# Cross attention of a Perceiver block: the spread as two rounded products, another order at the beginning, and one weight remainder on another engine

## What is computed

```python
x = x + xattn(layernorm(x), ctx)                 # x [32, 32, 512], ctx [32, 257, 512]
# inside xattn, 16 heads of 32:
q = x @ Wq + bq;  k, v = split(context @ Wkv + bkv)
q = larope(q);  k = larope(k)                    # rotation by position
scores = einsum('bhqd,bhkd->bhqk', q, k) * SCALE
attn = softmax(scores)                           # over 257 keys
out = einsum('bhqk,bhkd->bhqd', attn, v)         # back to [B, Lq, H * hd]
return out @ Wo + bo
```

## Time and profile before

| | us |
|---|---|
| median of 3 runs | 824.0 (823.18 to 825.72) |
| the profiled execution | 833.83 |
| its span, first to last instruction | 831.8 |
| PE busy in the span | 773.6 (93%) |
| VectorE, ScalarE, GpSimd busy | 459.1, 342.9, 211.7 |

### The profile page before, as it was taken

How to read it: one execution, slowest core, us unless ns; L and a number is a source line. 1 busy time by engine, 2 the same in 40 slices (tenths; PEclk the granted TensorE clock), 3 DMA queues, 4 the chain that set the end, 5 groups by cost and what they waited for, 6 DMA issues and landing times. The chain is left out here.

```text
span 831.8 us, 21082 instructions
## 1 busy us (share of the span) xinstructions
PE 773.6 (93%) x8896; PEld 645.1 (78%) x8897; DVE 459.1 (55%) x1005; ACT 342.9 (41%) x815; POOL 211.7 (25%) x194
## 2 busy tenths in 40 slices
PE   5889999999999999999999999999799996899980
PEld 4778888888898888888988888886577774678760
DVE  5645554554545546445555455555699985711115
ACT  6414335343353344433533445343466662123320
POOL 1212211231122212311232123121322220135540
PEclk9969999999999999999999999999899998589995
DMA  9503000010011000100010000213722329234438
GB/s 319 225 2 152 29 27 28 30 50 27 27 32 47 27 28 27 52 27 28 27 52 27 27 27 27 102 53 130 328 103 115 139 82 392 78 110 155 153 122 315
DMA packets 22249, 78.01 MB, mean 94 GB/s; under 512 B 3208, under 2 KB 3592, under 8 KB 19216
## 3 DMA queue, kind: packets, MB, share of 16 engines
q1 hardware_dynamic: 18480, 64.65, 20.9%
q0 software_dynamic: 3680, 12.06, 4.3%
HBM read 58.09 MB, written 18.61 MB: 92 GB/s over the span
## 5 line engine op out<-in xcount | busy, mean ns | idle before, releaser
L153 PE MATMUL bank<-chi,wparts 128*128 128x258 f32 x512 | 149.5, 292 | 7.6 <-DVE wparts L609 7.5
L154 PE MATMUL bank<-clo,wparts 128*128 128x258 f32 x512 | 145.3, 284 | 0.0
L155 PE MATMUL bank<-chi,wparts 128*128 128x258 f32 x512 | 145.3, 284 | 0.0
L153 PEld LDWEIGHTS bank<-chi,wparts 128*128 128x128 f32 x512 | 97.2, 190 | 20.4 <-issue 12.8
L314 POOL TENSOR_TENSOR ksin<-kb,const 128x1032 f32<-128x1032 f32 x32 | 95.1, 2971 | 62.8 <-ACT kb L373 62.8
L730 PE MATMUL bank<-wparts,chi 128*128 128x512 f32 x256 | 106.1, 414 | 0.2 <-DVE wparts L592 0.2
L731 PE MATMUL bank<-wparts,chi 128*128 128x512 f32 x256 | 101.5, 397 | 0.0
L732 PE MATMUL bank<-wparts,clo 128*128 128x512 f32 x256 | 101.3, 396 | 0.0
L320 POOL TENSOR_TENSOR pdiag<-pr,const 128x128 f32<-128x128 f32 x32 | 13.1, 410 | 340.7 <-ACT pr L381 340.7
L366 ACT ACTIVATE chi<-craw 128x1032 fp32r<-128x1032 f32 x32 | 34.1, 1066 | 157.3 <-PE bank L732 151.1
L154 PEld LDWEIGHTS bank<-clo,wparts 128*128 128x128 f32 x512 | 97.7, 191 | 0.0
(11 more groups left out here) (234 smaller groups left out, 1620.9 us busy)
## 6 DMA issues: line engine op xcount, KB each, us to landing
craw<-ctx_t_dram SPq DMA_DIRECT2D x32, 516.0 KB, 3.5
expert_lo<-weights_dram SPq DMA_DIRECT2D x8, 1024.0 KB, 12.0
expert_hi_scratch<-wraw SPq DMA_DIRECT2D x16, 512.0 KB, 2.6
wparts<-expert_hi_scratch SPq DMA_DIRECT2D x8, 1024.0 KB, 8.5
wraw<-weights_dram SPq DMA_DIRECT2D x7, 1024.0 KB, 6.7
expert_lo<-ffn_out_scratch SPq DMA_DIRECT2D x16, 256.0 KB, 4.6
x<-x_dram SPq DMA_DIRECT2D x8, 256.0 KB, 7.4
ffn_xn_scratch<-xn SPq DMA_DIRECT2D x8, 256.0 KB, 2.1
```

What stands on the lines that cost most here:

```text
L153: pe.matmul(psum, ahi(c), bhi(c), start=(c == 0), stop=False)
L154: pe.matmul(psum, ahi(c), blo(c), start=False, stop=False)
L155: last = pe.matmul(psum, alo(c), bhi(c), start=False, stop=(c == chunks - 1))
```

## The change

- The spread: the last probabilities and the inverse sums go into one tile `pair` of 128 x 8, VectorE splits it into a rounded part and a remainder (`pair_parts`), GpSimd's two diagonals are now those of the rounded part and of the remainder, each 128 x 256 of float32r, and PE adds two float32r products with a 0/1 matrix that GpSimd rounds once at the start (`same`).
- The beginning: VectorE first zeroes `kcos`, and PE makes 8 float32 products of 256 columns of it before its first work (`warm_up`). The first K goes chunk by chunk over all four parts, into four separate banks (`first_k_product`), and K's evacuations come after the roundings of Wq and Wv on ScalarE. Q and the first half of V wait chunk by chunk; both halves of V come before the transposes of rotated Q, whose halves are evacuated one by one. VectorE rotates Q before it makes kcos. SP issues Wv ahead of the bias of Q.
- The remainder of the output weight: not on GpSimd in batch 0 behind ksin, but on VectorE in batch 1, behind the remainder of transposed x (`w_lo(WO)`).
- Waits: the first exponential of a batch waits for the copies of `pair` in place of the diagonals; transposed Q counts two to a tile.

```diff
--- before.py
+++ after.py
...
     vlast = sb("vlast", [P, G, B])
-    pdiag = sb("pdiag", [P, 2, G, S])
+    pdiag = [sb(f"pdiag_{n}", [P, 2 * G, S], F32R) for n in ("hi", "lo")]
     olast = sb("olast", [P, G, S])
...
     rsum = sb("rsum", [P, G])
-    rinv = sb("rinv", [P, G])
+    pair = sb("p_last_and_rinv", [P, 2 * G])
+    pair_hi = sb("p_last_and_rinv_hi", [P, 2 * G], F32R)
+    pair_lo = sb("p_last_and_rinv_lo", [P, 2 * G])
+    same = sb("same_head", [P, P], F32R)
     pt = [sb(f"pt{i}", [P, 2 * P]) for i in range(G)]
...
     extra = score[3]
+    first_k = [proj[0], score[1], score[2], score[0]]
     av = quad[:, 3, 0:P]
...
     s_mask_rest = sem("mask_rest_in")
-    s_pdiag, s_spread, s_olast, s_osum, s_onorm = (sem(n) for n in (
+    s_pair_hi, s_pair_lo, s_same, s_pdiag, s_spread, s_olast, s_osum, s_onorm = (sem(n) for n in (
+        "p_last_and_rinv_hi_done", "p_last_and_rinv_lo_done", "same_head_rounded",
         "diagonals_done", "p_last_and_rinv_spread", "o_last_done", "o_sum_done", "o_normed"))
...
     sinq = const[:, C_SINQ:C_SINQ + 16].unsqueeze(1).to_broadcast([P, 2 * H, 16])
-    eye = const[:, C_EYE:C_EYE + S].unsqueeze(1).to_broadcast([P, G, S])
+    eye = const[:, C_EYE:C_EYE + S].unsqueeze(1).to_broadcast([P, 2 * G, S])
...
         weight(WQ)
+        weight(WV)
         bias_row(R_BQ, s_bq)
-        weight(WV)
         ctx(1, 1)
...
         def diagonals(b):
-            pool.wait_ge(s_exp, (b + 1) * G)
+            pool.wait_ge(s_pair_hi, b + 1)
             if not at_start(b):
                 pool.wait_ge(s_spread, b)
-            pool.tensor_tensor(pdiag[:, 0], pr[:, :, LK - 1].unsqueeze(2).to_broadcast([P, G, S]), eye, ALU.mult)
-            pool.wait_ge(s_rinv, b + 1)
-            pool.tensor_tensor(pdiag[:, 1], rinv[:].unsqueeze(2).to_broadcast([P, G, S]), eye,
+            pool.tensor_tensor(pdiag[0][:], pair_hi[:].bitcast(F32).unsqueeze(2).to_broadcast([P, 2 * G, S]), eye,
+                               ALU.mult)
+            pool.wait_ge(s_pair_lo, b + 1)
+            pool.tensor_tensor(pdiag[1][:], pair_lo[:].unsqueeze(2).to_broadcast([P, 2 * G, S]), eye,
                                ALU.mult).then_inc(s_pdiag, 1)
...
         pool.wait_ge(s_const, 16)
+        pool.tensor_copy(same[:], const[:, C_SAME:C_SAME + P]).then_inc(s_same, 1)
         ln_pool(pool, 0)
         k_sin(0)
-        def wo_lo():
-            pool.wait_ge(s_whi, WO)
-            pool.wait_ge(s_wlo, WO - 1)
-            pool.tensor_tensor(wlo[WO][:], wraw[WO % 2][:], whi[WO][:].bitcast(F32),
-                               ALU.subtract).then_inc(s_wlo, 1)
...
                     k_sin(b + 1)
-                if j == 0 and at_start(t):
-                    wo_lo()
...
                 act.wait_ge(s_ksin, b)
-            act.activation(kb[:, m, :], proj[m % 3][:, 0:LKP], ACT.Identity,
+            psum = first_k[m] if at_start(b) else proj[m % 3]
+            act.activation(kb[:, m, :], psum[:, 0:LKP], ACT.Identity,
                            bias=bias_cols[:, m:m + 1]).then_inc(s_kev, 1)
...
                 act.wait_ge(s_ptp, b * G)
-                act.wait_ge(s_pdiag, b)
+                act.wait_ge(s_rinv, 2 * b)
             act.activation(pr[:, g, 0:LK], sm[g][:], ACT.Exp, bias=nmax[:, g:g + 1], scale=-1.0,
...
         def qt_evac(t):
-            act.wait_ge(s_qtp, t + 1)
             if not at_start(t):
...
             for i in range(2):
+                act.wait_ge(s_qtp, 2 * t + i + 1)
                 act.activation(qt[i][:], score[2 + i].rearrange("p (g n) -> p g n", g=G),
...
         act.wait_ge(s_biask, 16)
-        k_evac(0, 0)
+        xt_hi(0)
         w_hi_chunks(WQ)
-        for m in range(1, 4):
+        w_hi_chunks(WV)
+        for m in range(4):
             k_evac(0, m)
-        xt_hi(0)
-        w_hi_chunks(WV)
         ctx_hi_at(0, 1)
...
             if not at_start(t):
-                dve.wait_ge(s_qtp, t)
+                dve.wait_ge(s_qtp, 2 * t)
             dve.tensor_tensor(qb[:], extra, bias[:, R_BQ, :], ALU.add).then_inc(s_qb, 1)
...
             if not at_start(b):
+                dve.wait_ge(s_pair_lo, b)
+            dve.reciprocal(pair[:, G:2 * G], rsum[:]).then_inc(s_rinv, 1)
+            dve.tensor_copy(pair[:, 0:G], pr[:, :, LK - 1]).then_inc(s_rinv, 1)
+        def pair_parts(b):
+            dve.wait_ge(s_rinv, 2 * b + 2)
+            if not at_start(b):
                 dve.wait_ge(s_pdiag, b)
-            dve.reciprocal(rinv[:], rsum[:]).then_inc(s_rinv, 1)
+            dve.tensor_copy(pair_hi[:], pair[:]).then_inc(s_pair_hi, 1)
+            dve.wait_ge(s_pair_hi, b + 1)
+            dve.tensor_tensor(pair_lo[:], pair[:], pair_hi[:].bitcast(F32), ALU.subtract).then_inc(s_pair_lo, 1)
...
                     dve.wait_ge(s_whi, n)
-                lo = dve.tensor_tensor(wlo[n][:, c, :], wraw[n % 2][:, c, :], whi[n][:, c, :].bitcast(F32),
-                                       ALU.subtract)
-            lo.then_inc(s_wlo, 1)
+                dve.tensor_tensor(wlo[n][:, c, :], wraw[n % 2][:, c, :], whi[n][:, c, :].bitcast(F32),
+                                  ALU.subtract).then_inc(s_wlo if c == KC - 1 else s_wklo, 1)
...
+        dve.memset(kcos[:], 0.0).then_inc(s_zero, 1)
         ctx_lo(0, 0)
...
         dve.wait_ge(s_x0, 16)
-        dve.wait_ge(s_zero, 1)
+        dve.wait_ge(s_zero, 2)
         ln(0, x[:, 0, :])
-        w_lo_chunks(WQ)
         dve.wait_ge(s_const, 16)
         xt_lo(0)
+        w_lo_chunks(WQ)
         w_lo_chunks(WV)
-        k_cos(0)
         dve.wait_ge(s_bq, 16)
         q_rope(0)
+        k_cos(0)
         ctx_lo(1, 1)
...
                 inverse_sums(b)
+                pair_parts(b)
                 if not (first and j == 0):
...
                     xt_lo(t + 1)
+                if j == 1 and first:
+                    w_lo(WO)
                 if j == 2 and not last:
...
+        def weight_chunk(n, c):
+            if c == KC - 1:
+                pe.wait_ge(s_wlo, n)
+            else:
+                pe.wait_ge(s_wklo, KC + (n - WQ) * (KC - 1) + c + 1)
         def q_product(t, b=None):
...
             mm3(pe, extra, lambda c: xthi[:, c, :], lambda c: xtlo[:, c, :],
-                lambda c: whi[WQ][:, c, :], lambda c: wlo[WQ][:, c, :]).then_inc(s_qmm, 1)
+                lambda c: whi[WQ][:, c, :], lambda c: wlo[WQ][:, c, :],
+                before=(lambda c: weight_chunk(WQ, c)) if at_start(t) else None).then_inc(s_qmm, 1)
...
             pe.wait_ge(s_qr, t + 1)
+            if at_start(t):
+                pe.wait_ge(s_kev, 3)
             if b is not None:
...
                     last = pe.transpose(score[2 + i][:, g * P:(g + 1) * P], a[:, g * P:(g + 1) * P], ident)
-            last.then_inc(s_qtp, 1)
-        def wk_chunk(c):
-            pe.wait_ge(s_wklo, c + 1)
+                last.then_inc(s_qtp, 1)
+        def warm_up():
+            pe.wait_ge(s_zero, 2)
+            for i in range(8):
+                pe.matmul(score[0][:, 0:2 * P], kcos[:, 0, 0:P], kcos[:, 1, 0:2 * P], start=True, stop=True)
+        def first_k_product():
+            pe.wait_ge(s_clo, 1)
+            for c in range(KC):
+                pe.wait_ge(s_wklo, c + 1)
+                for m in range(4):
+                    psum = first_k[m][:, 0:LKP]
+                    hi, lo = (a[:, c, m * P:(m + 1) * P] for a in (whi[WK], wlo[WK]))
+                    pe.matmul(psum, hi, chi[0][:, c, :], start=(c == 0), stop=False)
+                    pe.matmul(psum, hi, clo[0][:, c, :], start=False, stop=False)
+                    last = pe.matmul(psum, lo, chi[0][:, c, :], start=False, stop=(c == KC - 1))
+                    if c == KC - 1:
+                        last.then_inc(s_proj, 1)
...
                 pe.wait_ge(s_clo, b + 1)
-            if not (at_start(b) and m < 3):
-                if m == 0:
-                    pe.wait_ge(s_kev, b * 4)
-                elif m < 3:
-                    pe.wait_ge(s_vev, b * 2 - 2 + m)
-                else:
-                    pe.wait_ge(s_kev, b * 4 + 1)
+            if m == 0:
+                pe.wait_ge(s_kev, b * 4)
+            elif m < 3:
+                pe.wait_ge(s_vev, b * 2 - 2 + m)
+            else:
+                pe.wait_ge(s_kev, b * 4 + 1)
             mm3(pe, proj[m % 3][:, 0:LKP],
                 lambda c: whi[WK][:, c, m * P:(m + 1) * P], lambda c: wlo[WK][:, c, m * P:(m + 1) * P],
-                lambda c: chi[j % 2][:, c, :], lambda c: clo[j % 2][:, c, :],
-                before=wk_chunk if at_start(b) and m == 0 else None).then_inc(s_proj, 1)
+                lambda c: chi[j % 2][:, c, :], lambda c: clo[j % 2][:, c, :]).then_inc(s_proj, 1)
...
             psum = proj[(4 + u) % 3][:]
-            pe.wait_ge(s_kev, b * 4 + 2 + u)
+            if not at_start(b):
+                pe.wait_ge(s_kev, b * 4 + 2 + u)
             for c in range(KC):
+                if at_start(b) and u == 0:
+                    weight_chunk(WV, c)
```

(15 more changed lines are left out.)

## The result

The changed kernel takes 821.98 us (median of 20 runs, 818.03 to 824.69), the kernel before, measured with it on the same chip, 826.0 us (20 runs, 823.18 to 836.64). The ratio is 0.9942, 95% interval 0.9922 to 0.9962: about 4.8 us faster (the two medians are 4.0 apart). The direction was forecast, but the gain is half the size, and the time lies 3 us above the range. The ratios here leave out runs more than 1.5% above the fastest of their kernel, among them many of the long ones of the kernel before, so what is gained by ending long runs shows less in a ratio than in the mean of all runs. Of the 20 runs of the kernel before 7 lie above 831 us, of the kernel after none; the means are 828.8 and 822.0.

A forecast was written before the change was run, and what follows sets the result against it. PE, busy 100 of 100 us at full clock, was taken to bound the loop. Spread 6.4 plus batch 0 2.7 made 9.1 us, so 824.0 became 814.9 us; own range 811 to 817, 8-in-10 range 809 to 819.

The forecast's parts named there:

- The spread: On PE in the loop, two rounded products replace one float32 product: 0.20 us saved a batch, 6.4 us in all.
- The changeover of 0.10 us: On PE between the spread's last pass and attend: 0.10 us assumed to remain after the change.
- the bound of 9.0: Upper bound of the spread's saving, if the changeover belonged to the float32 pass: 0.28 us a batch, 9.0 us.
- The loop's other engines: Added VectorE and GpSimd work in the loop: hidden by about 8 us of slack, so 0 charged.
- rival D: In the loop, VectorE and GpSimd block each other and become the bound: slower, 830.4 us; chance 0.05.
- Rival C: In the loop, the spread's pair with changeovers costs 0.5 us and doesn't pay: 821.3 us; chance 0.08.
- the batch-0 term: Output weight remainder moved off GpSimd in batch 0: L644 ends at 42.4 instead of 45.13, gain 2.7 us (1.9 to 3.6).
- the forecast end of L644: VectorE's tiny subtraction in batch 0: starts at 42.05, takes 0.3 us without a lock, ends at 42.4.
- The beginning: Zero products and chunk-wise K, Q, V at the start: buys nothing, since exponentials wait for ctx 2; 0 charged, at worst 2.
- The term for the low clock behind the pause: PE in batch 0: 3.6 us pause still drops the clock; the low stretch from 45.18 to 56.82 repeats 2.7 us earlier.
- B: Batch 0 gains nothing, through a ctx 2 landing 2 us later or the lock; only the spread remains: 817.6 us; chance 0.12.
- A: In batch 0 the clock holds in PE's pause, 5.4 us more gained: 809.5 us; chance 0.15.

The follow-up runs named there:

- the kernel that always has it: Only the new beginning (zero products, chunk-wise first K, Q and V, new order) added to the kernel before: 833.39 us, ratio 1.0111.
- the one in which it is excluded: Kernel before plus one wait: GpSimd's ksin in batch 0 waits until VectorE has made xn of tile 1; 826.89 us, ratio 0.9988.
- the second trace of the changed kernel: The changed kernel run again without any edit, on the third chip: 823.25 us, ratio 0.9971 to the kernel before.
- the second trace of the kernel before: The kernel before run again unchanged, on the first chip: 826.84 us, ratio 1.003, trace span 822.5 us.
- the order forced: Changed kernel plus one wait: GpSimd's ksin in batch 0 waits until VectorE has made xn of tile 1; 820.27 us, ratio 0.9901.

## Why the prediction was half right

**The spread was right.** Forecast 0.20 us a batch and 6.4 in all. The eleven traces with the two products and the moved weight have a loop of 501.3 to 501.9 us (502.63 for the spread alone), the six with the float32 product one of 507.5 to 508.3. The changeover of 0.10 us that I kept is there, and the bound of 9.0 falls: it belongs to whatever comes before the attend, not to the float32 pass.

**The loop's other engines were right.** Nothing charged, and no wait shows. The widened diagonal takes 617 ns, where the sum had 0.67:

```profile
L325 POOL TENSOR_TENSOR pdiag_hi<-p_last_and_rinv_hi,const 128x256 fp32r<-128x256 f32 x32 | 19.7, 617 | 337.4 <-DVE p_last_and_rinv_hi L565 337.4
L492 DVE TENSOR_TENSOR clo<-craw,chi 128x1032 fp32r<-128x1032 f32 x32 | 51.7, 1617 | 3.5 <-ACT chi L364 3.5
```

The remainder of ctx (the second line) now takes 1617 ns on average instead of 1414: the diagonals hold it. PE has slack enough for it, so rival D never came near. Rival C is out too: the pair costs 0.33 us and not 0.5.

**The step that failed is the base of the batch-0 term.** I wrote that the output weight's move gains 2.7 us against the profiled 833.83, and carried the difference between that and the median over "unchanged". But those 9.8 us were not noise around one course of events. The earlier trace rows is the rarer of two orders: over the four chips 45 of 128 runs of the kernel before lie at or above 831 us, with a mean of 834.7; the other 83 have a mean of 825.6. The timed runs have no trace of their own; that the long ones are of this order is concluded from the kernel that always has it (832 to 836 us) and from the one in which it is excluded. The median run then has the other order, where L644 is held for 1.37 us and not for 4.58. Against that one the move alone gains about one microsecond, in the trace (attend 0 at 49.24 instead of 50.54) and in the mean of the runs (824.8 against 825.6). Inside the step the forecast end of L644 was met, 42.35 for 42.4, but by luck: ctx 2 landed 0.9 us later than before (32.42 for 31.53) and moved the exponentials, which I had fixed, by as much, while the added work on VectorE and GpSimd delayed rstd by about 0.7 and not by 1.5. Where ctx 2 landed at 31.55, in the second trace of the changed kernel, L653 ended at 41.5.

**The beginning: 7 us alone, nothing in company.** I charged 0 and "at worst 2". Alone it costs 7 us, because it makes the long order the rule; I had not priced the parts apart. Beside the moved weight its net cost can't be told from 0 (821.76 with it, 821.89 without). In the trace of the kernel after two losses are seen: the clock falls after a pause of 2.24 us that stands between chunk-wise K and Q, and the run from 18.1 to 21.5 at 1.2 GHz loses some 1.7 us, ahead of a transfer that is waited for anyway; and behind the pause at L653 3.4 us are lost between 45.4 and 52.2. The kernels without the new beginning lose to the clock in batch 0 as well. The term for the low clock behind the pause was of the right kind and mis-sized: the forecast had the small products at 1.2 GHz throughout, and they began at 2.4. Over the whole span the granted clock averages 0.9637 in the 83 shorter executions of before and 0.9593 in the changed kernel, so the changed kernel runs longer at the low clock than those do.

**The sum, mended by two traces.** From the forecast to the measured median are 7.1 us. The kernel before took 826.0 in the comparison and not 824.0: 2.0. Batch 0 and the beginning together are not 2.7 earlier but, in the two traces, 1.8 later (52.33 against 50.54): 4.5. The rest is 0.6. So 826.0 - 6.4 + 1.8 = 821.4 against 821.98 measured. In other executions of the changed kernel attend 0 started at 49.9 and 52.9, so the 1.8 is one draw, and that the sum closes so well is in part chance. It moves with the transfer of ctx 2, which landed between 29.5 and 33.0 in the traces; I had taken its moment as fixed.

**The rivals.** B (only the spread remains, 817.6) named the right outcome: in the median no more than the spread's gain can be seen. Its mechanism, a later ctx 2, had a part in the one trace (0.9 us), but it isn't why the gain in batch 0 was missing; the rarer order is. A was wrong in its form: the clock did hold through the pause and fell behind it. By A attend 0 would have started at 57.34 - 2.7 - 5.4 = 49.2; with the small remainder made early it started at 46.82 and 45.75.

**Left open.** From the last attend to the end, where no part of the change acts, the traces take 264 to 272 us. The six of kernels without the spread take 264.1 to 266.2, the eleven with spread and moved weight 264.3 to 271.6, on average 2.1 more; four of these, at 269.7 and above, have one more low-clock stretch of about 10 us between 710 and 726 us (so has the first trace of the kernel before, at 726 to 736, with an end of 266.2). This may be where part of the missing gain went, since attend 0 in the seven of them without the early remainder starts at 50.6 on average, against 50.54 in the second trace of the kernel before. Whether the change makes such ends more frequent, one trace of each kernel can't settle. Nor is it known why the clock falls where PE has had no pause, as at 46 us in the kernel before.

**The better version** in the timed runs is the changed kernel with the small remainder made at the start: 816.52 and 817.9 us on two chips, with ratios of 0.9887 and 0.9885 to the kernel before, some 5 us below the changed kernel beside it (6.7 and 3.9).

## What to carry to other kernels

Before a stall in one trace is priced, ask whether the median run has it. Where the profiled time lies well above the median (1.2% here), and two engines that hold each other up start within 0.1 us of each other, the trace may show the rarer order, and removing it pays only in those runs. A saving on the engine that bounds a loop multiplies as read (0.20 us 32 times), while a gain in a one-off chain ends at the next wait. A tiny operation that needs only early data (here 0.28 us on VectorE) belongs where nothing waits for it; moving it gave 6.7 and 3.9 us on two chips, about as much as the whole change.

## What the runs showed of the hardware

- A VectorE instruction of 128 elements a partition took 0.28, 1.37, 2.09 or 4.58 us, by which GpSimd instruction had started before it. A shift of 0.2 us separates the two traces of the kernel before, and its runs fall into a shorter and a longer kind (825.6 and 834.7 us on average).
- The clock fell from 2.4 to 1.2 GHz while PE was issuing products without a gap: at 45.4 us, after a pause of 2.14 had ended at 42.41, and at 18.1, after one of 2.24 had ended at 17.00. A pause ahead does not decide it alone. In batch 0 it fell in all eight traces with a pause of 0.33 us or more at the small products, and in six of the ten with 0.15 or none (in the kernel before near 46.0, in the one with spread, moved weight and early remainder at 46.0 too). The pause of 2.24 us in the beginning was followed by a fall within 1.3 us of its end in nine of the ten traces that have it; with the order forced it was not.
- Zero products from 1.97 to 8.6 us had K running at 2.4 GHz from its second product on (0.12 us apart). That bought nothing in the timed runs: leaving them out saved 2.8 us on one chip, and on another, with the remainder made early, 0.2.
